# Scan and weighing: one operand moved into PSUM in both

## The chip, the cores and the metric

The kernel runs on one core of one Trainium2 chip. The metric is the device time of one execution in microseconds. Five engines work side by side, each through its own list of instructions in order: TensorE (PE, with its weight loads as PEld), VectorE (DVE), ScalarE (ACT), GpSimd (POOL) and SyncE (SP, which issues most transfers). They meet through semaphores. SBUF is the working memory, PSUM the eight banks that TensorE writes into.

## The reference

Eight images of 56x56 pixels with 128 channels pass through four layers. Layers 0, 2 and 3 are deformable convolutions: for each pixel, 9 points in 4 groups are sampled from a table of projected pixels, each with 4 bilinear corners, weighted by corner and softmax mask, summed, projected, normalized, and sent through an MLP:

```
offset = (h @ w_off + b_off); mask = softmax(h @ w_msk + b_msk)
samp = sum over 4 corners of img[idx] * weight
y = einsum('nghwpc,nhwgp->nhwgc', samp, mask) @ w_out + b_out
x = x + gamma1 * layer_norm(y); x = x + gamma2 * layer_norm(mlp(x))
```

Layer 1 is a selective scan in four directions over the 3,136 pixels, with 256 channels (two halves of 128) and 16 states:

```
h = h * exp(dt * A) + (dt * u) * B
y = sum over the 16 states of h * C
```

## The kernel before

**Two strands of work.** The 24 stages (three deformable layers for eight images) and the scans of the eight images run interleaved. A planner writes one list of items before anything runs (`Planner`, `schedule`); each engine goes through that list and emits its share of each item. The planner alternates one weighing with some scan ticks at a fixed pace and places everything else (projections, depthwise convolutions, the MLP chain of pixel pairs) by lags counted in ticks. There is no other scheduling: an engine that waits holds up all that stands behind it in its list.

**A stage.** Pixels come in 25 tiles of 128. For each tile 36 points are gathered from a table in DRAM by GpSimd's indirect transfers (L730), one for each point, 128 rows of 128 numbers each (4 corners of 32 channels). Twelve of them form a third of a tile and fill one of five slots `d_g`. VectorE weighs a third when it has landed (L1325), in three instructions of four points, each gather times its weight `d_wt`, broadcast over 32 channels. TensorE then sums the 12 points and corners of the third by 24 matmuls with the identity into `d_p` (L1014; item `sum`, placed behind the first scan tick after the weighing). That frees the slot for GpSimd. A 24-point pair of tiles goes on through the MLP chain (item `ch`: L1188 to L1218 on TensorE, L1563 to L1587 on VectorE).

**The scan.** An image has 448 steps: 28 pieces (direction, stretch of 448 pixels) times 16 states. Each step has a tick `s`. For step S the decay exp(dt*A) is made by ScalarE for the first half of the channels into a PSUM bank (`dA0` in `l_pm`, L781) and for the second half into SBUF (`dA1`, three buffers). TensorE spreads the step's row of B over the partitions into bank `l_pb` and the row of C into `l_pc` (L965, one matmul each). VectorE's tick for step S, in order:
- L1288: scan of the first half, 448 pixels, decay from PSUM.
- L1290: scan of the second half, first 224 pixels, all operands in SBUF.
- L1301: `dtu` times B's row for step S+1, both halves, 896 elements, into one of four buffers `hb`. It frees `l_pb`.
- L1305: scan of the second half, last 224 pixels.
- L1311: `hb` of step S-1 times C's row, 896 elements. It frees `l_pc`.

TensorE's tick S: row of B for S+1 (item `sB`), row of C for S-1, then the accumulation of `hb` of step S-2 by four matmuls into `l_acc` (L996). ScalarE's tick saves the last column of step S-1 (`carry`, L762), makes dA1 for S+2 and dA0 for S+1. After the ticks of an image come items of its output (`g`, `m`) and the projection of the next one (`p`).

Of the kernel before, what the change touches and what calls it, by code (L numbers as in the profile page):

```python
# [10 lines left out]
ALU = mybir.AluOpType  # L11
# [7 lines left out]
C = 128  # L19
# [53 lines left out]
def vss_ticks(n, order):  # L73

    out = [(0.0, [("need", order.index((0, 0)))])] + after_scan(-1, n)
    for i in range(n):
        for c in range(2):
            for h in range(2):
                out += [(0.5, [("c", i, c, h, part)]) for part in range(3)]
        out += [(0.3, [("h", i, 0, m)]) for m in range(9)]  # L80
        for sig in range(-1, NSTEP + 3):
            tick = [("sB", i, sig - 1)] * (0 <= sig < NSTEP) + [("s", i, sig)]
            j, q = divmod(sig, 16)
            if 0 <= sig < NSTEP:
# [260 lines left out]
def bank_uses(item):  # L345
# [21 lines left out]
    if kind == "s":  # L367
        _, i, sig = item
        s = NSTEP * i + sig
        if sig == -1:  # L370
            return [("pb", ("B", s + 1))]
        return [("pc", ("C", s - 1))] if 1 <= sig <= NSTEP else []
    if kind == "sB":
        _, i, sig = item
        return [("pb", ("B", NSTEP * i + sig + 2))] if sig + 2 < NSTEP else []
# [22 lines left out]
class Mem:  # L398


    def __init__(self, sb, ps, dram, n):
# [82 lines left out]

        self.dA0, self.dA1 = self.pm[:, 0:448], [wk[5][:, 0, :], wk[5][:, 1, :], wk[6][:, 0, :]]
# [26 lines left out]
class Job:  # L512


    def __init__(self, n, order, plan, mem, sems, a, out):
# [11 lines left out]
        self.total = total  # L527

# [217 lines left out]
def scalar_program(e, J):  # L746
# [211 lines left out]
def tensor_program(e, J):  # L958
# [17 lines left out]
    for item in J.plan:  # L976
        kind = item[0]
        if kind == "s":
            _, i, sig = item
            S = NSTEP * i + sig  # L980
            if sig == -1:
# [16 lines left out]
        elif kind == "sB":  # L998
            _, i, sig = item
            if sig + 2 < NSTEP:  # L1000
                row_of_B(NSTEP * i + sig + 2)
# [224 lines left out]
def vector_program(e, J):  # L1226
# [30 lines left out]
    for item in J.plan:  # L1257
        kind = item[0]
        if kind == "s":
# [17 lines left out]
            if 0 <= sig < NSTEP:  # L1277
# [5 lines left out]
                way, one, two, mid = slice(None), slice(0, 224), slice(224, 448), 223  # L1283
                if kd >= 2:
                    way, one, two, mid = slice(None, None, -1), slice(447, 223, -1), slice(223, None, -1), 224
                e.wait_ge(s["f_pb"], J.free("B", S))
# [20 lines left out]
            if 1 <= sig <= NSTEP:  # L1307
                x = S - 1
                e.wait_ge(s["p_pc"], J.full("C", x))
                e.wait_ge(s["ca"], x + 1)  # L1310
                e.tensor_tensor(m.hb[x % 4][:, :, :], m.hb[x % 4][:, :, :], bc(m.pc[:, 0:448], 1, 2),  # L1311
                                ALU.mult).then_inc(s["f_pc"], 1)
        elif kind == "weigh":
# [232 lines left out]
        elif kind == "ch":  # L1546
# [48 lines left out]
         "dA0 dA1 s1h sh ca accd d1 d2 hd0 md m2 lo ab ex uu qq s1 ln pag psq xir brd lag lsq xmr gsq gt gb tg").split()  # L1595
# [106 lines left out]
```

## Time and profile before

| | us |
|---|---|
| median of 3 runs | 31,024.93 |
| lowest, highest | 30,998.21, 31,036.17 |
| span of the profiled execution | 31,070.8 |
| VectorE busy | 23,050.6 (74%) |
| TensorE busy | 23,014.3 (74%) |
| GpSimd busy | 23,383.1 (75%) |
| ScalarE busy | 12,015.2 (39%) |

The profiled execution is the span and is 46 us over the median of the runs. Busy time counts instructions, not the issue time between two gathers, so GpSimd's share is to be read with its idle time beside it. The first scan tick starts at about 1,605 us and the last ends at about 28,258 us; before and after there are only stages.

### The profile page before, as it was taken

Reading aid. Unit: us, or ns where it says so; the run is one execution under the profiler, and the core shown is the slowest. Engines: PE = TensorE matmul, PEld = TensorE weight load, DVE = VectorE, ACT = ScalarE, POOL = GpSimd, SP = SyncE. Lnnn points to the kernel's source line nnn. Section 1 sums busy time; section 2 is a strip of 40 time slices with the busy share of each in tenths; the row PEclk is TensorE's granted clock in tenths of the full one; section 3 lists DMA queues with packets and bytes.
Section 4 is the critical chain, followed back from the end, with each engine's and each line's share of the span. In section 5 each row is a group of like instructions: output and inputs, shape, how many; then the busy total and the mean of one; then the engine's idle time right before and its main releaser. Section 6 shows DMA issues by size and latency. Waiting matters only on the chain.

```text
span 31070.8 us, 287429 instructions
## 1 busy us (share of the span) xinstructions
PE 23014.3 (74%) x94224; PEld 14570.5 (47%) x94224; DVE 23050.6 (74%) x38816; ACT 12015.2 (39%) x20358; POOL 23383.1 (75%) x21172
## 2 busy tenths in 40 slices
PE   5578778787787778777877787777877787777444
PEld 4444445444544454444544454444544454435433
DVE  1289887888588868888788859886788858885212
ACT  1144444444344434443444434443444444433000
POOL 6777777777677777777777767777677777656767
PEclk7788889888888888888988889888888888888666
DMA  3212122221221221212222121212222121112221
GB/s 75 75 50 64 54 66 65 57 64 51 71 61 51 64 73 51 64 50 57 70 58 63 49 72 53 59 51 64 58 58 61 50 72 52 51 42 67 64 57 53
DMA packets 2410662, 1854.55 MB, mean 60 GB/s; under 512 B 1686546, under 2 KB 2045508, under 8 KB 2409164
## 3 DMA queue, kind: packets, MB, share of 16 engines
q0 software_dynamic: 677376, 1388.62, 16.1%
q1 hardware_dynamic: 1731788, 447.55, 6.5%
q8 instruction: 745, 12.21, 0.2%
q14 instruction: 753, 6.17, 0.1%
HBM read 1569.35 MB, written 265.21 MB: 59 GB/s over the span
## 4 chain that ended last, share of the span: by engine, by line
POOL 61%; issue 18%; PE 12%; DVE 6%; ACT 2%; DMA 1%; SPq 1%; DVEq 0%; POOLq 0%; ACTq 0%
POOL d_g L730 61%; PE d_p L1014 2%; PE d_pr L1162 2%; DVE l_wk L1311 1%; PE l_acc L996 1%; DVE l_wk L1288 1%; DVE d_g L1325 1%; PE d_pr L1049 1%; PE l_pc L1127 1%; DVE l_wk L1305 1%; PE d_pr L1216 1%; DMA d_xin<-mid 0%; SPq L629 0%; DVE l_wk L1290 0%; PE d_pr L1209 0%
## 5 line engine op out<-in xcount | busy, mean ns | idle before, releaser
L730 POOL DMA_INDIRECT d_g<-table,d_idx x21168 | 23382.9, 1105 | 7645.0 <-issue 6426.9
L1014 PE MATMUL d_p<-d_g,c_ident 128*128 128x128 f32 x43200 | 6292.8, 312 | 2702.1 <-DVE d_g L1325 2697.1
L1014 PEld LDWEIGHTS d_p<-d_g,c_ident 128*128 128x128 f32 x43200 | 6108.4, 226 | 3849.1 <-DVE d_g L1325 2820.6
L996 PE MATMUL l_acc<-l_wk,c_ident 128*128 128x448 f32 x14336 | 7295.8, 639 | 436.7 <-DVE l_yx L1276 348.4
L1325 DVE TENSOR_TENSOR d_g<-d_g,d_wt 128x512 f32<-128x512 f32 x5304 | 3361.9, 689 | 3335.2 <-DMA d_g<-table,d_idx 3333.1
L781 ACT ACTIVATE l_pm<-l_wk,l_a 128x448 f32<-128x448 f32 x3584 | 2272.9, 634 | 7292.9 <-DVE l_wk L1288 7287.8
L1301 DVE TENSOR_TENSOR l_wk<-l_wk,l_pb 128x896 f32<-128x896 f32 x3584 | 3824.5, 1067 | 1501.6 <-PE l_pb L965 1499.4
L996 PEld LDWEIGHTS l_acc<-l_wk,c_ident 128*128 128x128 f32 x14336 | 3176.0, 223 | 2507.2 <-issue 2334.0
L1311 DVE TENSOR_TENSOR l_wk<-l_wk,l_pc 128x896 f32<-128x896 f32 x3584 | 3808.2, 1063 | 25.3 <-ACT l_carry L762 21.1
L1288 DVE TENSOR_TENSOR_SCAN l_wk<-l_pm,l_carry,l_wk 128x448 f32<-128x448 f32 x3072 | 3505.4, 1141 | 4.2 <-ACT l_pm L781 1.6
L1305 DVE TENSOR_TENSOR_SCAN l_wk<-l_wk 128x224 f32<-128x224 f32 x3584 | 2432.1, 679 | 0.3
L781 ACT ACTIVATE l_wk<-l_wk,l_a 128x448 f32<-128x448 f32 x3584 | 2362.2, 659 | 17.1 <-DVE l_wk L1357 3.0
L965 PE MATMUL l_pc<-l_spl,c_sel 96*128 96x448 bf16 x3584 | 1424.5, 397 | 1190.4 <-DVE l_wk L1311 1184.1
L1290 DVE TENSOR_TENSOR_SCAN l_wk<-l_wk,l_carry 128x224 f32<-128x224 f32 x3072 | 2026.0, 659 | 0.0
L965 PE MATMUL l_pb<-l_spl,c_sel 96*128 96x448 bf16 x3584 | 1400.9, 391 | 670.5 <-DVE l_wk L1301 668.7
L762 ACT ACTIVATE l_carry<-l_wk 128x2 f32<-128x2 f32 x3584 | 725.9, 203 | 2695.8 <-DVE l_wk L1305 2689.5
L781 ACT ACT_TABLE_LOAD x1181 | 1515.2, 1283 | 21.2
L1162 PE MATMUL d_pr<-d_xt,d_diag 128*128 128x448 f32 x3024 | 1358.5, 593 | 33.9 <-ACT d_xt L889 27.0
L1216 PE MATMUL d_pr<-d_fc,d_ht 128*128 128x128 f32 (+1 forms) x4800 | 903.8, 347 | 546.3 <-ACT d_ht L950 546.2
L965 PEld LDWEIGHTS l_pc<-l_spl,c_sel 96*128 96x128 bf16 x3584 | 369.2, 103 | 1902.7 <-DVE l_wk L1311 1754.3
L1216 PEld LDWEIGHTS d_pr<-d_fc,d_ht 128*128 128x128 f32 (+1 forms) x4800 | 771.6, 242 | 768.5 <-ACT d_ht L950 712.8
L965 PEld LDWEIGHTS l_pb<-l_spl,c_sel 96*128 96x128 bf16 x3584 | 370.2, 103 | 1597.6 <-DVE l_wk L1301 1104.1
(178 smaller groups left out, 22691.0 us busy)
## 6 DMA issues: line engine op xcount, KB each, us to landing
d_g<-table,d_idx POOLq DMA_INDIRECT x21168
table<-d_pst SPq DMA_DIRECT2D x2376, 64.0 KB
hd<-d_hst SPq DMA_DIRECT2D x168, 224.0 KB
d_htc<-hd SPq DMA_DIRECT2D x144, 256.0 KB
d_xin<-mid SPq DMA_DIRECT2D x112, 224.0 KB
mid<-d_xo SPq DMA_DIRECT2D x192, 128.0 KB
d_xres<-mid SPq DMA_DIRECT2D x192, 128.0 KB, 2.2
d_xin<-in_x SPq DMA_DIRECT2D x56, 224.0 KB
```

The costliest lines, as they stand in the source:

```text
L730: e.indirect_dma_start(out=m.g[Q % SLOTS][:, j, :], out_offset=None, in_=m.table[k % 2], in_offset=bass.IndirectOffsetOnAxis(ap=m.idx[G % ...
L781: e.activation(m.dA0 if h == 0 else m.dA1[x % 3], m.dt[P % 2][:, h, :], ACT.Exp, scale=m.aa[:, kd, h, n:n + 1]).then_inc(s[f"dA{h}"], 1)
L965: return e.matmul(bank[:, 0:448], m.sel[:, row + n:row + n + 1].to_broadcast([96, 128]), m.spl[P % 2][:, :], start=True, stop=True)
L996: ins = e.matmul(m.acc[:, h, 0:448], m.ident[:, :], m.hb[x % 4][:, h, :], start=(n == 0), stop=(n == 15))
L1014: ins = e.matmul(m.p0[:, t % 2 * 128:t % 2 * 128 + 32 * w], m.ident[:, :], m.g[Q % SLOTS][:, w * p:w * p + w, 32 * r:32 * r + 32], start=( ...
L1216: e.matmul(bank[0:n, i * 128:i * 128 + 128], m.ht[:, f, i * n:i * n + n], m.fc2[:, f, :], start=(f == 0), stop=False)
L1288: e.tensor_tensor_scan(hb[:, 0, way], m.dA0[:, way], hb[:, 0, way], ini[0], ALU.mult, ALU.add).then_inc(s["sh"], 1)
L1290: e.tensor_tensor_scan(hb[:, 1, one], dA1[:, one], hb[:, 1, one], ini[1], ALU.mult, ALU.add).then_inc(s["s1h"], 1)
L1301: e.tensor_tensor(m.hb[x % 4][:, :, :], m.dtu[P % 2][:, :, :], bc(m.pb[:, 0:448], 1, 2), ALU.mult).then_inc(s["f_pb"], 1)
L1305: e.tensor_tensor_scan(hb[:, 1, two], dA1[:, two], hb[:, 1, two], hb[:, 1, mid:mid + 1], ALU.mult, ALU.add).then_inc(s["sh"], 1)
L1311: e.tensor_tensor(m.hb[x % 4][:, :, :], m.hb[x % 4][:, :, :], bc(m.pc[:, 0:448], 1, 2), ALU.mult).then_inc(s["f_pc"], 1)
L1325: ins = e.tensor_tensor(g, g, wt, ALU.mult)
```

## The change

The second half's scan becomes one instruction of 448 that reads its input from B's bank `l_pb` in PSUM. For that the product of step S+1 is made in two instructions: the first half goes into `hb` as before, the second half is written over B's row in `l_pb`. The bank is free again only when that scan has read it. VectorE's order in a tick is now: scan of the first half, scan of the second half, product by C (S-1), two products by B (S+1). TensorE's item `sB` is gone: the tick spreads C's row for S-1 first, then B's row for S+1, then accumulates.

For a weighing that is the first after a scan tick (and whose weights were ready when that tick was written), ScalarE copies the weights of the third, 128x48, into the unused columns 448 to 496 of the bank `l_pm` at the end of its tick. VectorE weighs the third in one instruction of 1,536 elements with the weights read from there. Other weighings stay as they are.

```diff
-            tick = [("sB", i, sig - 1)] * (0 <= sig < NSTEP) + [("s", i, sig)]
+            tick = [("s", i, sig)]
...
+        self.wps = self.pm[:, 448:496]
...
+    def find_weights_in_psum(self):
+
+        self.copied, self.from_psum = {}, {}
+        step, ready = None, set()
+        for item in self.plan:
+            if item[0] == "s":
+                step, ready_then = item[1:], set(ready)
+            elif item[0] == "pr" and item[3] == 11:
+                ready.add(item[1:3])
+            elif item[0] == "weigh" and step and 0 <= step[1] < NSTEP - 1 and step not in self.copied:
+                if (item[1], item[2] // 4) in ready_then:
+                    self.copied[step] = item[1:]
+                    self.from_psum[item[1:]] = len(self.copied)
...
ScalarE, tick:
-                e.wait_ge(s["sh"], 2 * S)
+                e.wait_ge(s["sh"], S)
+                e.wait_ge(s["f_pb"], J.free("B", S - 1))
...
+            if (i, sig) in J.copied:
+                k, t, u = J.copied[i, sig]
+                G = 7 * k + t // 4
+                w = 4 * THIRDS[t][u]
+                e.wait_ge(s["wtr"], G + 1)
+                e.activation(m.wps[:, 0:w], m.wt[G % 2][:, t % 4, 12 * u:12 * u + THIRDS[t][u]].rearrange("p j r -> p (j r)"),
+                             ACT.Copy).then_inc(s["wps"], 1)
...
TensorE, tick:
-            if sig == -1:
-                row_of_B(S + 1)
             if 1 <= sig <= NSTEP:
                 if J.use["C", S - 1]:
                     e.wait_ge(s["f_pc"], J.use["C", S - 1])
                 spread(S - 1, m.pc, 16).then_inc(s["p_pc"], 1)
+            if sig + 1 < NSTEP:
+                row_of_B(S + 1)
...
VectorE, tick:
+                row = m.pb[:, 0:448]
+                e.wait_ge(s["bm"], 2 * S + 1)
                 e.wait_ge(s["dA0"], S + 1)
                 e.tensor_tensor_scan(hb[:, 0, way], m.dA0[:, way], hb[:, 0, way], ini[0], ALU.mult, ALU.add).then_inc(s["sh"], 1)
+                e.wait_ge(s["bm"], 2 * S + 2)
                 e.wait_ge(s["dA1"], S + 1)
-                e.tensor_tensor_scan(hb[:, 1, one], dA1[:, one], hb[:, 1, one], ini[1], ALU.mult, ALU.add).then_inc(s["s1h"], 1)
+                e.tensor_tensor_scan(hb[:, 1, way], dA1[:, way], row[:, way], ini[1], ALU.mult, ALU.add).then_inc(s["f_pb"], 1)
...
                 e.wait_ge(s["p_pb"], J.full("B", x))
-                e.tensor_tensor(m.hb[x % 4][:, :, :], m.dtu[P % 2][:, :, :], bc(m.pb[:, 0:448], 1, 2),
-                                ALU.mult).then_inc(s["f_pb"], 1)
-            if 0 <= sig < NSTEP:
-                e.wait_ge(s["s1h"], S + 1)
-                e.tensor_tensor_scan(hb[:, 1, two], dA1[:, two], hb[:, 1, two], hb[:, 1, mid:mid + 1],
-                                     ALU.mult, ALU.add).then_inc(s["sh"], 1)
+                e.tensor_tensor(m.hb[x % 4][:, 0, :], m.dtu[P % 2][:, 0, :], m.pb[:, 0:448], ALU.mult).then_inc(s["bm"], 1)
+                e.tensor_tensor(m.pb[:, 0:448], m.dtu[P % 2][:, 1, :], m.pb[:, 0:448], ALU.mult).then_inc(s["bm"], 1)
...
VectorE, weighing:
+            if (k, t, u) in J.from_psum:
+                e.wait_ge(s["wps"], J.from_psum[k, t, u])
+            step = parts if (k, t, u) in J.from_psum else 4
+            for j in range(0, parts, step):
+                if (k, t, u) in J.from_psum:
+                    wt = bc(m.wps[:, 0:4 * parts], 2, 32)
...
                 ins = e.tensor_tensor(g, g, wt, ALU.mult)
```

## Rows read from the trace of the kernel before

**Rows 1.** The page, part 4: the chain that ended last, by engine.
```profile
POOL 61%; issue 18%; PE 12%; DVE 6%; ACT 2%; DMA 1%; SPq 1%; DVEq 0%; POOLq 0%; ACTq 0%
```

**Rows 2.** Busy time (count) of PE, PEld, DVE, ACT, POOL in the scan stretch, granted clock, DMA share, GB/s.
```profile
1605.00:28258.00 26653.00, 20676.05 (x83559) 12671.17 (x83559) 22063.76 (x35990) 11464.66 (x19471) 20323.44 (x17985) 0.86 0.22 59
```

**Rows 3.** Grouped instructions of GpSimd, scan stretch and tail: busy, mean ns | idle, releasers.
```profile
L730 POOL DMA_INDIRECT d_g<-table,d_idx x17985 | 20323.7, 1130 | 6329.8 <-issue 5459.4 <-DVE d_idx L1520 494.8 <-PE d_p L1014 375.6
L730 POOL DMA_INDIRECT d_g<-table,d_idx x2039 | 1957.4, 960 | 814.0 <-issue 619.0 <-DVE d_idx L1520 154.6 <-PE d_p L1014 40.4
```

**Rows 4.** Grouped instructions of VectorE in the scan stretch.
```profile
L1301 DVE TENSOR_TENSOR l_wk<-l_wk,l_pb 128x896 f32<-128x896 f32 x3583 | 3823.4, 1067 | 1497.6 <-PE l_pb L965 1495.4
L1311 DVE TENSOR_TENSOR l_wk<-l_wk,l_pc 128x896 f32<-128x896 f32 x3582 | 3806.0, 1063 | 23.0 <-ACT l_carry L762 21.1 <-PE l_pc L965 1.6
L1288 DVE TENSOR_TENSOR_SCAN l_wk<-l_pm,l_carry,l_wk 128x448 f32<-128x448 f32 x3072 | 3505.4, 1141 | 4.2 <-ACT l_pm L781 1.6
L1325 DVE TENSOR_TENSOR d_g<-d_g,d_wt 128x512 f32<-128x512 f32 x4513 | 2854.1, 687 | 1063.2 <-DMA d_g<-table,d_idx 1061.2
L1305 DVE TENSOR_TENSOR_SCAN l_wk<-l_wk 128x224 f32<-128x224 f32 x3584 | 2432.1, 679 | 0.3
L1290 DVE TENSOR_TENSOR_SCAN l_wk<-l_wk,l_carry 128x224 f32<-128x224 f32 x3072 | 2026.0, 659 | 0.0
```

**Rows 5.** Grouped matmuls of TensorE in the scan stretch.
```profile
L996 PE MATMUL l_acc<-l_wk,c_ident 128*128 128x448 f32 x14324 | 7291.0, 639 | 436.7 <-DVE l_yx L1276 348.4 <-DVE l_yx L1271 88.3
L1014 PE MATMUL d_p<-d_g,c_ident 128*128 128x128 f32 x35304 | 4805.5, 299 | 949.7 <-DVE d_g L1325 944.9
L965 PE MATMUL l_pc<-l_spl,c_sel 96*128 96x448 bf16 x3582 | 1423.8, 397 | 1190.4 <-DVE l_wk L1311 1184.1
L965 PE MATMUL l_pb<-l_spl,c_sel 96*128 96x448 bf16 x3582 | 1400.2, 391 | 670.1 <-DVE l_wk L1301 668.3
```

**Rows 6.** Timeline, 16,510 to 16,525 us: start, us, engine, instruction, idle before.
```profile
16510.46 0.68 DVE L1305 TENSOR_TENSOR_SCAN l_wk<-l_wk 128x224 f32<-128x224 f32 x1
...
16510.62 1.27 POOL L730 DMA_INDIRECT d_g<-table,d_idx  x1 [0.30 <-issue]
...
16515.36 1.14 DVE L1288 TENSOR_TENSOR_SCAN l_wk<-l_pm,l_carry,l_wk 128x448 f32<-128x448 f32 x1
...
16515.49 5.03 PE L1014 MATMUL d_p<-d_g,c_ident 128*128 128x128 f32 x24 [0.61 <-DVE d_g L1325]
...
16517.21 0.95 POOL L730 DMA_INDIRECT d_g<-table,d_idx  x1 [0.31 <-issue]
...
16520.71 1.14 DVE L1288 TENSOR_TENSOR_SCAN l_wk<-l_pm,l_carry,l_wk 128x448 f32<-128x448 f32 x1
...
16521.60 1.67 PE L996 MATMUL l_acc<-l_wk,c_ident 128*128 128x448 f32 x4
...
16524.90 1.14 DVE L1288 TENSOR_TENSOR_SCAN l_wk<-l_pm,l_carry,l_wk 128x448 f32<-128x448 f32 x1
```

**Rows 7.** Timeline, 10,004 to 10,017 us.
```profile
10004.28 2.84 PE L1014 MATMUL d_p<-d_g,c_ident 128*128 128x128 f32 x24
...
10015.60 1.08 DVE L1349 SCALAR_TENSOR_TENSOR l_wk<-l_wk 128x896 f32<-128x896 f32 x1
...
10015.77 3.55 POOL L730 DMA_INDIRECT d_g<-table,d_idx  x1 [0.30 <-issue]
...
10016.60 1.89 DVE L1325 TENSOR_TENSOR d_g<-d_g,d_wt 128x512 f32<-128x512 f32 x3
```

**Rows 8.** Other forms, grouped over the whole span: VectorE, then ScalarE.
```profile
L1353 DVE TENSOR_TENSOR l_wk<-l_wk 128x896 f32<-128x896 f32 x224 | 243.0, 1085 | 0.1
L1271 DVE SCALAR_TENSOR_TENSOR l_yx<-l_xb,l_ds,l_acc 128x448 f32<-128x448 f32 x112 | 70.7, 673 | 0.0
...
L762 ACT ACTIVATE l_carry<-l_wk 128x2 f32<-128x2 f32 x3584 | 725.9, 203 | 2695.8 <-DVE l_wk L1305 2689.5
L781 ACT ACTIVATE l_pm<-l_wk,l_a 128x448 f32<-128x448 f32 x3584 | 2272.9, 634 | 7292.9 <-DVE l_wk L1288 7287.8
```

More of the change, by code:

```diff
@@ L369, in bank_uses @@
         s = NSTEP * i + sig
-        if sig == -1:
[L371 to L375, printed above, removed]
+        uses = [("pc", ("C", s - 1))] if 1 <= sig <= NSTEP else []
+        return uses + [("pb", ("B", s + 1))] if sig + 1 < NSTEP else uses
     if kind == "g":
@@ L527, in __init__ @@
         self.total = total
+        self.find_weights_in_psum()
+    def find_weights_in_psum(self):
[10 more added lines that the diff above has]
+                    self.from_psum[item[1:]] = len(self.copied)
     def tables(self, T):
@@ L777, in scalar_program @@
                 if h == 0 and x:
-                    e.wait_ge(s["sh"], 2 * x - 1)
+                    e.wait_ge(s["sh"], x)
                 if h == 1 and x >= 3:
-                    e.wait_ge(s["sh"], 2 * x - 4)
+                    e.wait_ge(s["f_pb"], J.free("B", x - 3))
                 e.activation(m.dA0 if h == 0 else m.dA1[x % 3], m.dt[P % 2][:, h, :], ACT.Exp,
                              scale=m.aa[:, kd, h, n:n + 1]).then_inc(s[f"dA{h}"], 1)
+            if (i, sig) in J.copied:
[5 more added lines that the diff above has]
+                             ACT.Copy).then_inc(s["wps"], 1)
         elif kind == "h":
@@ L980, in tensor_program @@
             S = NSTEP * i + sig
-            if sig == -1:
-                row_of_B(S + 1)
             if 1 <= sig <= NSTEP:
@@ L997, in tensor_program @@
                 ins.then_inc(s["accd"], 1)
[L998 to L1001, printed above, removed]
         elif kind == "sum":
@@ L1281, in vector_program @@
                 ini = [0.0 if c == (6 if kd >= 2 else 0) else m.carry[:, h, n:n + 1] for h in range(2)]
[L1283 to L1286, printed above, removed]
+                way = slice(None, None, -1) if kd >= 2 else slice(None)
+                row = m.pb[:, 0:448]
+                e.wait_ge(s["bm"], 2 * S + 1)
                 e.wait_ge(s["dA0"], S + 1)
                 e.tensor_tensor_scan(hb[:, 0, way], m.dA0[:, way], hb[:, 0, way], ini[0], ALU.mult, ALU.add).then_inc(s["sh"], 1)
+                e.wait_ge(s["bm"], 2 * S + 2)
                 e.wait_ge(s["dA1"], S + 1)
-                e.tensor_tensor_scan(hb[:, 1, one], dA1[:, one], hb[:, 1, one], ini[1], ALU.mult, ALU.add).then_inc(s["s1h"], 1)
+                e.tensor_tensor_scan(hb[:, 1, way], dA1[:, way], row[:, way], ini[1], ALU.mult, ALU.add).then_inc(s["f_pb"], 1)
+            if 1 <= sig <= NSTEP:
+                x = S - 1
+                e.wait_ge(s["p_pc"], J.full("C", x))
+                e.wait_ge(s["ca"], x + 1)
+                e.tensor_tensor(m.hb[x % 4][:, :, :], m.hb[x % 4][:, :, :], bc(m.pc[:, 0:448], 1, 2),
+                                ALU.mult).then_inc(s["f_pc"], 1)
             if sig + 1 < NSTEP:
@@ L1300, in vector_program @@
                 e.wait_ge(s["p_pb"], J.full("B", x))
-                e.tensor_tensor(m.hb[x % 4][:, :, :], m.dtu[P % 2][:, :, :], bc(m.pb[:, 0:448], 1, 2),
-                                ALU.mult).then_inc(s["f_pb"], 1)
-            if 0 <= sig < NSTEP:
-                e.wait_ge(s["s1h"], S + 1)
-                e.tensor_tensor_scan(hb[:, 1, two], dA1[:, two], hb[:, 1, two], hb[:, 1, mid:mid + 1],
-                                     ALU.mult, ALU.add).then_inc(s["sh"], 1)
[L1307 to L1312, printed above, removed]
+                e.tensor_tensor(m.hb[x % 4][:, 0, :], m.dtu[P % 2][:, 0, :], m.pb[:, 0:448], ALU.mult).then_inc(s["bm"], 1)
+                e.tensor_tensor(m.pb[:, 0:448], m.dtu[P % 2][:, 1, :], m.pb[:, 0:448], ALU.mult).then_inc(s["bm"], 1)
         elif kind == "weigh":
@@ L1321, in vector_program @@
             e.wait_ge(s[name], count)
-            for j in range(0, parts, 4):
-                g = m.g[Q % SLOTS][:, j:min(j + 4, parts)].rearrange("p j (r c) -> p (j r) c", c=32)
-                wt = bc(m.wt[G % 2][:, t % 4, 12 * u + j:12 * u + min(j + 4, parts)].rearrange("p j r -> p (j r)"), 2, 32)
+            if (k, t, u) in J.from_psum:
+                e.wait_ge(s["wps"], J.from_psum[k, t, u])
+            step = parts if (k, t, u) in J.from_psum else 4
+            for j in range(0, parts, step):
+                g = m.g[Q % SLOTS][:, j:min(j + step, parts)].rearrange("p j (r c) -> p (j r) c", c=32)
+                if (k, t, u) in J.from_psum:
+                    wt = bc(m.wps[:, 0:4 * parts], 2, 32)
+                else:
+                    wt = bc(m.wt[G % 2][:, t % 4, 12 * u + j:12 * u + min(j + 4, parts)].rearrange("p j r -> p (j r)"), 2, 32)
                 ins = e.tensor_tensor(g, g, wt, ALU.mult)
@@ L1594 @@
          "weighed accq ysa ytp yta idx wtr w0 pv py exd bst agg sqd x1r xor gbr dgr bsq bnr "
-         "dA0 dA1 s1h sh ca accd d1 d2 hd0 md m2 lo ab ex uu qq s1 ln pag psq xir brd lag lsq xmr gsq gt gb tg").split()
+         "wps dA0 dA1 bm sh ca accd d1 d2 hd0 md m2 lo ab ex uu qq s1 ln pag psq xir brd lag lsq xmr gsq gt gb tg").split()
 def program(nc, a, out, n_img=8, layers=(0, 1, 2, 3)):
```

## The prediction

> **What bounds the kernel now.** I read the chain of waits first: 61% of it is GpSimd's gathers and 18% the issue time between them [rows 1], so the reader should suspect GpSimd, not VectorE. Then three stretches: 0 to 1,605 us (no scans yet), 1,605 to 28,258 us (the 3,584 ticks of the scan beside the gathers), and the rest. In the middle one, the scan stretch, VectorE is busy 22,064 of 26,653 us, TensorE 20,676, GpSimd 20,323 [rows 2]. GpSimd looks freer than it is: its 17,985 gathers have 5,459 us of issue time between them (0.30 each) and only 870 us of real waits [rows 3]. It is 97% taken. A gather takes 1,130 ns there, but 960 ns in the tail, where VectorE does little [rows 3]. So something on VectorE lengthens it.
>
> The grouped instructions of VectorE say how little slack it has against GpSimd: it waits 1,061 us for gathers (1,063 idle in all) (before weighings) and 1,498 us for B's row from TensorE (before L1301) in this stretch [rows 4]. All three engines are within a few per cent of each other; that is the difficulty of this case.
>
> The timeline shows what lengthens gathers. One that starts 1.85 us into a tick, where the product L1301 with its row in PSUM runs, takes 0.95 us; one that meets L1305 takes 1.27 [rows 6], and one that meets L1349 and the three weighings takes 3.55 and ends within about 1 us of them [rows 7]. L1305, L1290, L1325 and L1349 have two SBUF inputs. Gathers wait for such instructions and not for those with an operand in PSUM.
>
> **Part 1, the weighings.** A weighing of 12 points is three instructions of 512 elements: 1.89 us [rows 7]. It becomes one of 1,536 with the weights in PSUM. Counted in the written order, 1,347 of 1,776 weighings qualify (one after each scan tick that has one); the rest lie at the stage ends, the head and the tail. Price: 896 elements take 1.067 us at L1301, 512 take 0.687 at L1325 and 896 all in SBUF 1.085 at L1353 [rows 4, 8], 1.03 ns an element, so 1.067 + 640 x 1.03 ns = 1.73 us. That saves 0.16 us, and with the seams between three instructions I take 0.2 x 1,347 = 270 us of VectorE (bounds: -100, if the repeated read from PSUM is slower than L1301's, to 300).
>
> ScalarE gets 1,347 copies of 128x48: between 0.20 us (128x2) and 0.63 (128x448) [rows 8], taken as 0.25, 340 us in all. They are queued behind dA0 of the next step, which starts when the first scan ends; VectorE has 3 us of its tick left then, and ScalarE is busy 11,465 of 26,653 us [rows 2]. I cost them at nothing; without that cover they would cost up to 340 us.
>
> **Part 2, the scan's second half.** Per tick L1290 and L1305 (0.659 + 0.679) become one scan of 448, which at L1288 takes 1.141 [rows 4]: -0.20. The product of 896 (1.067) becomes two of 448: 2 x (1.067 - 0.461) = 1.21 by the same slope, and at most 2 x 0.673 by L1271 [rows 8], +0.14 to +0.28, the second writing into PSUM, which no row shows. Instructions overlap by some 0.08 us, which takes a little off both. Sum -0.06 x 3,584 = -200 us (bounds -250 to +300; I take the near row's).
>
> A page would put these otherwise. The Trainium skill ("VectorE: DVE Perf Modes", the TRN2 errata section) gives instructions from PSUM a fixed cost 62 cycles above those from SBUF, 65 ns at 0.96 GHz. Here the opposite stands: L1311 with a PSUM operand takes 1.063, L1353 all in SBUF 1.085 [rows 4, 8], so the measurement decides; by the page the two parts would give back 0.065 x (3,584 + 1,347) = 320 us of the 470.
>
> **What GpSimd gets.** L1290, L1305 and nine tenths of L1325 no longer have two SBUF inputs; L1349, L1353 and their like stay. In the tail, where only weighings are of that kind, gathers take 0.96 us [rows 3]; beside a single L1305 they lose 0.32 [rows 6]. I bound the new mean of the stretch by 0.96 and 1.05, which frees 1,400 to 3,000 us of GpSimd over 17,985 gathers, and take the middle, 2,200. It then needs some 2,200 us less than the stretch is long, and is off the path. So VectorE loses its waits for gathers, 1,063 us. This is the purpose, and by itself it makes 1,063 + 270 + 200 = 1,530 us.
>
> **What it costs: B's row.** Before, the bank of B's row comes free at the end of the product L1301, and the next row is read a tick later after the first scans: TensorE may be a whole tick early. After, the bank carries the product and comes free only when the scan of the second half ends. Then TensorE (in order: C's row, B's row, the two accumulations, the sum of a weighing, pieces of convolutions and of the MLP) must write B's row while VectorE does one product by C (1.06 us). The row itself is hidden, 0.39 us [rows 5]. But everything queued behind it waits for that scan's end too, every tick, and TensorE can bank no lead. Behind it stand the accumulations, the sums (which free gather slots; five slots, so GpSimd bears that), and the chain of the MLP. And C's row, now ahead of B's, must be there before the product.
>
> So each tick costs the longer of TensorE's work between two B rows and VectorE's work; light ticks no longer pay for heavy ones. In the written order a weighing is always followed by a scan tick, and its sum of 24 matmuls comes in that next tick; 1,349 ticks have a sum and none of these has a weighing. TensorE's heavy ticks are VectorE's light ones.
> - TensorE in a tick with a sum, mean rows [rows 5]: B 0.39, accumulation 7,291/3,582 = 2.04, sum 4,806/1,471 = 3.27, C 0.40, the rest (20,676 less these four groups, over 3,584) 1.6: 7.7 us. At full clock: accumulation 1.67, sum 2.84 [rows 6, 7], the two rows 0.6 together and the rest 1.35 (estimates: the means of above at that clock, overlapping): 6.45.
> - VectorE in such a tick: 4.19 for the scan tick (16,520.71 to 16,524.90, a tick with nothing else in it) [rows 6], and 0.75 for the rest (22,064 less the groups of rows 4, over 3,584): 4.95.
> - The excess is 1.5 to 2.75 us. The example of rows 6 by hand: second scan ends at 17.5 instead of TensorE running free, B's row to 17.9, accumulation to about 20, sum to 23 to 25, L1209 and C's row to 24.1 to 26.2, where VectorE wants it at 22.8: 1.4 to 3.4 us late. Today that tick has no stall.
>
> I take the middle, 2.1 us x 1,349 = 2,830 us. Of today's 1,498 us of stalls I count half as lying on such ticks already and keep the other half, 750. Stalls after: 3,580, which is 2,080 more than today. The granted clock decides within this: 0.86 in the stretch [rows 2], and sums that follow a wait run at the lower of the two levels, 1.2 GHz (5.03 us, after a wait for the weighing [rows 6]), those behind other work at 2.4 (2.84 [rows 7]).
>
> **Sum.** +2,080 - 1,063 - 470 = +550 us on the profiled execution, whose span is 31,071 us; the median shown is 31,025, 46 lower, and I take the difference as it is: 31,570 less something for TensorE being found closer to its upper clock level once sums no longer wait for their weighing: **31,500 us**, about 1.5% slower. Head and tail (4,418 us) keep their SBUF weighings and do not change.
>
> **Rivals.**
> - Faster: the lead TensorE loses was not used. For it: GpSimd's relief is certain, and TensorE waits 1,184 us for L1311 before C's row [rows 5], so it has idle time somewhere. Against: that idle time lies in ticks without a sum and cannot be moved. If stalls stay at 1,498 us: 31,025 - 1,530 = 29,500; if they grow half as much, 30,500. The Trainium skill ("SBUF — State Buffer", on the port pair that VectorE and GpSimd share) has the rule by which only this gain would show: an instruction with two SBUF inputs locks GpSimd out for its whole length. The rows above agree on the lock; it says nothing of TensorE. Chance 0.33.
> - Near nothing: gain and stalls cancel at an excess of 1.7 us a tick: 31,000. Chance 0.13.
> - Much slower: the excess is 2.75 us and all of today's stalls remain: the stalls grow by 1,349 x 2.75 = 3,710 us, less 1,530: +2,180, 33,200. TensorE's waits in the MLP chain would have to be just as long as now although it comes later. Chance 0.10 for over 32,500.
> - The change frees nothing: gathers stay at 1.13 us because it is another thing that delays them. Then GpSimd keeps its 97%, and TensorE's stalls partly coincide with waits for gathers: -470 - 1,063 is not to be had in full, about 32,000. Chance 0.04, on the slower side.
> - Likeliest, 31,100 to 32,500: chance 0.40.
>
> The sign turns at one point: whether TensorE's tick with a sum exceeds VectorE's by more or less than 1.7 us. A measurement of this kernel can tell 0.2% (60 us) from no change. Faster 0.33, same 0.13, slower 0.54. The range for 8 in 10 is 29,900 to 32,500; the likeliest case alone has 31,100 to 32,300.
>
> **What would show it.** Gathers in the scan stretch at 1.00 us instead of 1.13; GpSimd with real waits of 2 ms or more, now for TensorE's sums (slots). Waits for gathers before weighings below 200 us. VectorE waiting 3 ms or more for B's and C's rows, mostly in the tick after a weighing. The one-instruction weighing at 1.73, the second scan at 1.14, the products at 0.60 each. Wrong if: waits for rows stay under 2,500 us (then it is faster), the product into PSUM takes over 0.8 us, or weighings wait for ScalarE's copy.

## The result, and where the time went

The changed kernel takes 32,746 us (median of 4 runs, 32,739 to 32,763) against 31,024 for the kernel before: a ratio of 1.0556 (95% interval 1.0541 to 1.0571). It is slower, as forecast, but by 1,720 us where I had 475, and outside the range.

The profiled execution has a span of 32,737.3 us. First the chain that ended last, by engine, from the page of the changed kernel; it answers to [rows 1].

```profile
PE 44%; DVE 30%; issue 13%; POOL 8%; ACT 4%; DMA 1%; SPq 1%; DVEq 0%; ACTq 0%; POOLq 0%
```

GpSimd's share went from 61% to 8%, and TensorE's from 12% to 44%. The scan stretch, now from 1,604 to 29,941 us, with the columns of [rows 2], and GpSimd's gathers in it, answering to [rows 3]:

```profile
1604.00:29941.00 28337.00, 21371.52 (x83525) 13092.33 (x83526) 21753.38 (x33316) 11575.74 (x20819) 17609.65 (x18022) 0.82 0.22 55
...
L742 POOL DMA_INDIRECT d_g<-table,d_idx x18022 | 17610.3, 977 | 10727.6 <-issue 5211.0 <-PE d_p L1030 4281.9 <-DVE d_idx L1538 1234.7
```

The gather fell from 1,130 to 977 ns, GpSimd's work in the stretch from 20,323 to 17,610 us, and its real waits rose from 870 to 5,517 us, most of them for slots that TensorE's sums free. All that the change did for GpSimd became idle time. Now VectorE's groups in the same stretch, answering to [rows 4]:

```profile
L1311 DVE TENSOR_TENSOR l_wk<-l_wk,l_pc 128x896 f32<-128x896 f32 x3582 | 3839.2, 1072 | 4465.3 <-PE l_pc L985 3644.1 <-ACT l_carry L775 817.9
L1303 DVE TENSOR_TENSOR_SCAN l_wk<-l_pm,l_carry,l_wk 128x448 f32<-128x448 f32 x3072 | 3498.2, 1139 | 4.5 <-ACT l_pm L794 1.7
L1306 DVE TENSOR_TENSOR_SCAN l_wk<-l_wk,l_carry,l_pb 128x448 f32<-128x448 f32 x3072 | 3437.1, 1119 | 0.0
L1343 DVE TENSOR_TENSOR d_g<-d_g,l_pm 128x1536 f32<-128x1536 f32 x1329 | 2314.0, 1741 | 8.8 <-ACT l_pm L801 6.5
L1324 DVE TENSOR_TENSOR l_pb<-l_wk,l_pb 128x448 f32<-128x448 f32 x3584 | 2224.3, 621 | 0.0
L1323 DVE TENSOR_TENSOR l_wk<-l_wk,l_pb 128x448 f32<-128x448 f32 x3583 | 2191.9, 612 | 17.0 <-PE l_pb L985 16.8 <-issue 0.2
```

The new instructions cost what the rows of before said: second scan 1.12 us, products 0.61 and 0.62, weighing 1.74. The product into PSUM is 9 ns dearer than the one into SBUF. What is new is 4,465 us of idle time before the product by C (L1311), where there were 23; the 1,498 us before the product by B (L1301) have become 17 (L1323). Who waits for whom, over the whole span of the changed kernel (engine, line, waited for: us, times, longest):

```profile
PE l_pb L985 <- DVE l_wk L1306: 5570.0, 2046, 10.6
...
POOL d_g L742 <- PE d_p L1030: 4355.2, 922, 43.6
DVE l_wk L1311 <- PE l_pc L985: 3651.0, 1249, 12.9
...
ACT l_wk L824 <- PE d_pr L1052: 1585.2, 424, 12.5
ACT l_bcd L812 <- PE d_pr L1044: 1290.7, 224, 12.7
```

TensorE waits 5,570 us for the second scan before it may write B's row, in 2,046 of 3,584 ticks; VectorE waits 3,651 us for C's row, in 1,249. Neither engine is full. Counted tick by tick in the trace, 1,356 of the 3,584 ticks have the sum of a weighing in TensorE's list between two C rows, and these carry 3,035 us of the waits for C's row; the other 2,228 ticks carry 616. Before the change the waits for B's row split into 868 and 627. So the new stalls lie where TensorE's tick is heavy and VectorE's light. The timeline shows one round of it (start, us, engine, instruction, idle before):

```profile
16515.43 1.11 DVE L1306 TENSOR_TENSOR_SCAN l_wk<-l_wk,l_carry,l_pb 128x448 f32<-128x448 f32 x1
...
16516.60 0.56 PE L985 MATMUL l_pb<-l_spl,c_sel 96*128 96x448 bf16 x1 [5.63 <-DVE l_wk L1306]
...
16516.95 3.19 PE L1016 MATMUL l_acc<-l_wk,c_ident 128*128 128x448 f32 x4
...
16519.79 1.12 DVE L1306 TENSOR_TENSOR_SCAN l_wk<-l_wk,l_carry,l_pb 128x448 f32<-128x448 f32 x1
...
16520.08 2.13 PE L1044 MATMUL d_pr<-l_xb,l_xp 128*40 128x448 f32 x4
...
16522.14 2.94 PE L1030 MATMUL d_p<-d_g,c_ident 128*128 128x128 f32 x24
16522.24 0.54 ACT L812 ACTIVATE l_bcd<-d_pr 40x448 f32<-40x448 f32 x1 [6.06 <-PE d_pr L1044]
...
16523.32 0.19 ACT L775 ACTIVATE l_carry<-l_wk 128x2 f32<-128x2 f32 x1
...
16524.92 0.35 PE L985 MATMUL l_pc<-l_spl,c_sel 96*128 96x448 bf16 x1
...
16525.31 1.09 DVE L1311 TENSOR_TENSOR l_wk<-l_wk,l_pc 128x896 f32<-128x896 f32 x1 [4.40 <-PE l_pc L985]
```

TensorE idles 5.63 us until the scan L1306 ends at 16,516.54. Only then come B's row, the accumulation at the lower clock level (granted clock 0.50 from 16,516.6 to 16,520; 3.19 us for what takes 1.67 at 1.00 [rows 6]), an item of the next piece's prelude (L1044, the projection from which the piece's rows of B and C come) and the sum. C's row is there at 16,525.27; VectorE had wanted it at 16,520.9. The same lines show a wait that I had not priced: ScalarE's list stands at L812 for TensorE's L1044 until 16,522.24, and `carry` (L775) stands behind it. The product by C needs `carry` too: it overwrites the `hb` of step S-1, whose last column `carry` saves.

The stretch closes by these terms: VectorE's time at work, overlaps counted once, -310 us (22,064 to 21,753); waits for gathers -1,057 (1,061 to 4); waits for rows +2,164 (1,497 to 3,661); waits for `carry` +797 (21 to 818); all other waits of VectorE, together, +90. Sum +1,684; head and tail -17; span +1,667.

One of these terms misleads. The profile puts a wait down to whatever ended it last. In 218 of the 302 ticks in which `carry` came last C's row was late too, and only some 255 of the 818 us lie after its arrival. Had `carry` always been in time, VectorE would have waited for C's row through the other 560 or so (worked out from the end times in the trace, not from a run).

### The profile page after: what moved, and what is told of

It reads as the page before. It is cut to its first block, busy times and chain, and to the rows that moved or that the text cites. A ratio compares the mean times of both kernels' runs of the same rounds, so it can differ in the third digit from the quotient of the medians.

```text
span 32737.3 us, 294488 instructions
## 1 busy us (share of the span) xinstructions
PE 23709.4 (72%) x94224; PEld 14986.9 (46%) x94224; DVE 22735.6 (69%) x36140; ACT 12125.6 (37%) x21705; POOL 20626.5 (63%) x21172
## 4 chain that ended last, share of the span: by engine, by line
PE 44%; DVE 30%; issue 13%; POOL 8%; ACT 4%; DMA 1%; SPq 1%; DVEq 0%; ACTq 0%; POOLq 0%
PE d_p L1030 13%; PE l_acc L1016 12%; POOL d_g L742 8%; DVE l_wk L1306 6%; DVE l_wk L1303 6%; DVE d_g L1343 4%; DVE l_wk L1323 3%; DVE l_wk L1311 3%; PE d_pr L1178 3%; PE l_pb L985 2%; PE d_pr L1065 2%; PE d_pr L1044 2%; PE d_pr L1232 1%; DVE l_pb L1324 1%; PE d_pr L1225 1%
## 5 line engine op out<-in xcount | busy, mean ns | idle before, releaser
L742 POOL DMA_INDIRECT d_g<-table,d_idx x21168 | 20626.3, 974 | 12068.1 <-issue 6166.5
L1016 PE MATMUL l_acc<-l_wk,c_ident 128*128 128x448 f32 x14336 | 8172.8, 705 | 0.0
L1030 PEld LDWEIGHTS d_p<-d_g,c_ident 128*128 128x128 f32 x43200 | 6327.5, 231 | 2924.3 <-DVE d_g L1343 1586.1
L1311 DVE TENSOR_TENSOR l_wk<-l_wk,l_pc 128x896 f32<-128x896 f32 x3584 | 3841.4, 1072 | 4472.3 <-PE l_pc L985 3651.0
L1016 PEld LDWEIGHTS l_acc<-l_wk,c_ident 128*128 128x128 f32 x14336 | 3477.3, 243 | 2164.0 <-issue 2005.4
L1306 DVE TENSOR_TENSOR_SCAN l_wk<-l_wk,l_carry,l_pb 128x448 f32<-128x448 f32 x3072 | 3437.1, 1119 | 0.0
L1343 DVE TENSOR_TENSOR d_g<-d_g,d_wt 128x512 f32<-128x512 f32 x1281 | 812.2, 688 | 2264.4 <-DMA d_g<-table,d_idx 2264.2
L1343 DVE TENSOR_TENSOR d_g<-d_g,l_pm 128x1536 f32<-128x1536 f32 x1347 | 2330.9, 1730 | 8.8 <-ACT l_pm L801 6.5
L1324 DVE TENSOR_TENSOR l_pb<-l_wk,l_pb 128x448 f32<-128x448 f32 x3584 | 2224.3, 621 | 0.0
L1323 DVE TENSOR_TENSOR l_wk<-l_wk,l_pb 128x448 f32<-128x448 f32 x3584 | 2192.5, 612 | 20.8 <-PE l_pb L985 20.7
L1232 PE MATMUL d_pr<-d_fc,d_ht 128*128 128x128 f32 (+1 forms) x4800 | 814.1, 322 | 238.2 <-ACT d_ht L970 236.1
L1584 DVE BATCH_NORM_STATS2 d_bs<-d_pr 128x6 f32<-128x128 f32 (+1 forms) x1200 | 294.4, 284 | 916.6 <-PE d_pr L1234 709.5
L1232 PEld LDWEIGHTS d_pr<-d_fc,d_ht 128*128 128x128 f32 (+1 forms) x4800 | 708.4, 223 | 445.0 <-ACT d_ht L970 365.7
```

Source lines behind the costliest of these rows:

```text
L742: e.indirect_dma_start(out=m.g[Q % SLOTS][:, j, :], out_offset=None, in_=m.table[k % 2], in_offset=bass.IndirectOffsetOnAxis(ap=m.idx[G % ...
L1016: ins = e.matmul(m.acc[:, h, 0:448], m.ident[:, :], m.hb[x % 4][:, h, :], start=(n == 0), stop=(n == 15))
L1030: ins = e.matmul(m.p0[:, t % 2 * 128:t % 2 * 128 + 32 * w], m.ident[:, :], m.g[Q % SLOTS][:, w * p:w * p + w, 32 * r:32 * r + 32], start=( ...
L1306: e.tensor_tensor_scan(hb[:, 1, way], dA1[:, way], row[:, way], ini[1], ALU.mult, ALU.add).then_inc(s["f_pb"], 1)
L1323: e.tensor_tensor(m.hb[x % 4][:, 0, :], m.dtu[P % 2][:, 0, :], m.pb[:, 0:448], ALU.mult).then_inc(s["bm"], 1)
L1324: e.tensor_tensor(m.pb[:, 0:448], m.dtu[P % 2][:, 1, :], m.pb[:, 0:448], ALU.mult).then_inc(s["bm"], 1)
```

## Experiments

The first four ran on one chip in one session, beside 31,029 us for the kernel before; the next four in another beside 31,014. "Row stalls" are VectorE's waits for B's or C's row over the span.

**The weighings alone** (e1_weights): the kernel before with this part of the change.

```diff
+        self.wps = self.pm[:, 448:496]
+            if (i, sig) in J.copied:   # ScalarE's copy, as in the change
-            for j in range(0, parts, 4):
+            step = parts if (k, t, u) in J.from_psum else 4
+            for j in range(0, parts, step):
```

> The kernel before with the weighings of the change alone (weights copied into PSUM, one instruction of 1,536); the scan and the order of TensorE are as before. My theory (the loss is the held bank of B's row and what TensorE loses by it): this part is a gain by itself. VectorE loses 0.16 us x 1,347 = 215 us of work, gathers fall from 1,130 to about 1,075 ns in the scan stretch, waits for rows stay near 1,500 us, VectorE's waits for gathers fall below 400 us: 29.9 to 30.6 ms. Rival (ScalarE's copies, or the read of the weights from PSUM, delay VectorE): 31.0 ms or more, with VectorE waiting for ScalarE before C's product by several hundred us.

Measured: 30,032 us, ratio 0.9684 (0.9667 to 0.9700). Gathers in its scan stretch and VectorE's weighings and products over the span:

```profile
L746 POOL DMA_INDIRECT d_g<-table,d_idx x17986 | 18859.8, 1049 | 6728.1 <-issue 5431.1 <-DVE d_idx L1549 719.2 <-PE d_p L1037 577.8
```

```profile
L1324 DVE TENSOR_TENSOR l_wk<-l_wk,l_pb 128x896 f32<-128x896 f32 x3584 | 3814.0, 1064 | 1593.2 <-PE l_pb L988 1590.4
L1334 DVE TENSOR_TENSOR l_wk<-l_wk,l_pc 128x896 f32<-128x896 f32 x3584 | 3794.2, 1059 | 36.4 <-ACT l_carry L778 23.6 <-PE l_pc L988 12.6
L1354 DVE TENSOR_TENSOR d_g<-d_g,l_pm 128x1536 f32<-128x1536 f32 x1329 | 2313.4, 1741 | 56.6 <-DMA d_g<-table,d_idx 43.0 <-ACT l_pm L804 7.6 <-issue 4.0
```

Half of the change is a gain of 3.2% by itself. Waits for gathers in the stretch fell to 90 us, row stalls stayed (1,603), ScalarE's copies cost 8 us of waits. The rival falls. The gathers' relief was larger than I expected (1,049, not 1,075 ns); why was not tested.

**The scan alone** (e2_scan): the changed kernel with the weighings of before.

```diff
         self.copied, self.from_psum = {}, {}
+        return
```

> The changed kernel with its weighings put back as they were before (three instructions from SBUF); only the scan's part of the change stays. My theory: the whole loss is here. Waits of VectorE before the product by C for C's row near 3,600 us and for ScalarE's carry near 800 us, as in the changed kernel; 32.8 to 33.3 ms, above the changed kernel, since the weighings cost 200 us more and lengthen gathers, though those are off the path. Rival (the weighings carry a good part of the loss): 31.5 to 32.3 ms.

Measured: 32,909 us, ratio 1.0608 (1.0591 to 1.0626). Row stalls 3,661, waits for `carry` 805, nearly as in the changed kernel (3,672 and 818). The whole loss is here, and with it in place the weighings are worth 160 us instead of 1,000: waits for gathers are down to 10 us in the stretch without them, so there is nothing left for them to save there.

**The hold alone** (e4_hold): the kernel before, VectorE untouched, TensorE made to write B's row after C's and not before the tick's first scan has ended.

```diff
-            if sig == -1:
-                row_of_B(S + 1)
...
                 spread(S - 1, m.pc, 16).then_inc(s["p_pc"], 1)
+            if sig + 1 < NSTEP:
+                if sig >= 0:
+                    e.wait_ge(s["sh"], 2 * S + 1)
+                row_of_B(S + 1)
```

> The kernel before with the hold alone: TensorE writes C's row first and then B's row, and B's row waits for the first scan (L1288) of the same tick. VectorE's instructions, their operands and the weighings are as before. My theory: VectorE's waits for rows rise from 1,500 to 3,500 us or more although no instruction of VectorE changed; its waits for gathers vanish (1,060 us); 31.8 to 32.8 ms. Rival (TensorE's lead was not used; the loss comes from the new instructions on VectorE): 31.0 to 31.2 ms.

Measured: 32,438 us, ratio 1.0453 (1.0435 to 1.0470). The same views, VectorE's group over the span and then the two waits:

```profile
L1295 DVE TENSOR_TENSOR l_wk<-l_wk,l_pb 128x896 f32<-128x896 f32 x3584 | 3873.6, 1081 | 3757.6 <-PE l_pb L961 3666.9
```

```profile
PE l_pb L961 <- DVE l_wk L1282: 4087.1, 1981, 9.6
DVE l_wk L1295 <- PE l_pb L961: 3666.9, 1405, 13.2
```

Not one instruction of VectorE is changed, and the stalls at B's row go from 1,499 to 3,667 us, 2,933 of them in ticks with a sum. Its waits for gathers in the stretch vanish as well (2 us), though nothing relieves GpSimd. The hold makes most of the loss: 1,409 us, where the whole scan part (e2_scan) loses 1,880. The edit also puts C's row ahead of B's, as the change does; the two were not tried apart. `carry` cost 19 us here. In this order VectorE waits for TensorE at the product by B and does one more scan before it wants `carry`; that this is what covers ScalarE's delay was only argued.

**The hold removed** (e3_two): e2_scan with two banks for B's row.

```diff
+def bank_of(x):
+    return ("pb", "pm")[x % 2]
-        self.dA0, self.dA1 = self.pm[:, 0:448], [...]
+        self.dA0, self.dA1 = wk[6][:, 1, :], [...]
-            e.wait_ge(s["f_pb"], J.use["B", x])
+            e.wait_ge(s["f_" + bank_of(x)], J.use["B", x])
-                row = m.pb[:, 0:448]
+                row = (m.pb, m.pm)[S % 2][:, 0:448]
```

> e2_scan with two banks for B's row, pb for even and pm for odd steps; dA0 moves from pm into SBUF to make room, so the first scan has two SBUF inputs and the second one operand in PSUM. VectorE's order and TensorE's order are those of e2_scan; only the wait of B's row for the scan of the same tick becomes one for the scan a tick earlier. My theory: VectorE's waits for rows fall from about 3,600 to under 1,500 us and the wait for the carry to under 200; gathers are longer again (about 1,110 ns) and GpSimd bounds: 30.5 to 31.2 ms. Rival (VectorE's new order, two long scans and then C's product, needs C's row too early whatever the banks do): waits before C's product stay over 3,000 us and the time over 32 ms.

Measured: 30,217 us, ratio 0.9741 (0.9725 to 0.9757), below the range that I gave. Gathers, and the product by C, over the span:

```profile
L747 POOL DMA_INDIRECT d_g<-table,d_idx x21168 | 22384.2, 1057 | 7778.7 <-issue 6410.8
...
L1316 DVE TENSOR_TENSOR l_wk<-l_wk,l_pc 128x896 f32<-128x896 f32 x3584 | 3811.6, 1064 | 1502.9 <-PE l_pc L990 1174.1
```

VectorE's list is the one of e2_scan; only where the first scan's decay lies and which scan B's row waits for differ. 2,690 us come back. Row stalls are 1,188, fewer than before the change (1,503); in ticks with a sum they are 659 us. The wait for `carry` fell to 324, not under 200, where e1_weights has 24; so a part of it does not come from the hold, and which piece of the edit makes it was not tested. I had the gathers too long: 1,075 ns in the stretch, not 1,110. That one block of some 1.1 us a tick delays them less than two of 0.66 does not explain it: e8_merge below has one block too, and its gathers are no shorter than those of e1_weights.

**When TensorE is let go, and what is queued behind it** (e5_swap, e6_acc, e7_swap_acc): the changed kernel with VectorE's two scans exchanged; with the accumulation ahead of B's row; with both.

```diff
 VectorE (e5, e7)
+                e.wait_ge(s["bm"], 2 * S + 2)
+                e.wait_ge(s["dA1"], S + 1)
+                e.tensor_tensor_scan(hb[:, 1, way], ...).then_inc(s["f_pb"], 1)
                 e.wait_ge(s["dA0"], S + 1)
                 e.tensor_tensor_scan(hb[:, 0, way], ...).then_inc(s["sh"], 1)
 TensorE (e6, e7)
-            if sig + 1 < NSTEP:
-                row_of_B(S + 1)
             if 2 <= sig <= NSTEP + 1:
...
                 ins.then_inc(s["accd"], 1)
+            if sig + 1 < NSTEP:
+                row_of_B(S + 1)
```

> The changed kernel with VectorE's two scans exchanged: the second half's scan, which frees the bank of B's row, comes first in the tick, so TensorE is let go 1.06 us earlier while VectorE needs C's row and B's row at the same places as before. My theory (the loss is how late TensorE is let go, set against its work in a tick): the waits before C's product fall from 3,650 + 820 us by up to 1.06 us for each of the 1,249 late ticks, to 2,900 to 3,500 us together; 31.3 to 32.0 ms. Rival (TensorE's lower clock level makes the loss, not the time of release): stalls and time as in the changed kernel within 1%.

> The changed kernel with TensorE's accumulation of step S-2 (L1016, four matmuls) put ahead of B's row instead of behind it. Its work in a tick is the same, but less of it is queued behind the hold, and only B's row, wanted 1.06 us after C's, comes last. My theory: each late tick gains 0.4 to 1.0 us, stalls fall by 500 to 1,200 us, now split between C's product and the product by B: 31.5 to 32.3 ms. Rival (the same work between two releases gives the same stalls): within 0.5% of the changed kernel.

> Both of the above together. If they act on the same lateness one after the other, the gains add up: 30.7 to 31.4 ms, about the time of the kernel before. If one takes what the other would have taken: as the better of the two, 31.3 ms or more.

| kernel | us | ratio (95%) | C's row | B's row | carry |
|---|---|---|---|---|---|
| changed | 32,746 | 1.0556 | 3,651 | 21 | 818 |
| e5_swap | 31,438 | 1.0132 (1.0115 to 1.0149) | 2,589 | 17 | 613 |
| e6_acc | 31,692 | 1.0218 (1.0201 to 1.0235) | 1,766 | 1,196 | 403 |
| e7_swap_acc | 31,171 | 1.0046 (1.0030 to 1.0063) | 1,337 | 1,171 | 349 |

The last three columns are VectorE's waits in us over the span. Exchanging two neighbouring instructions on VectorE gives 1,308 us, the earlier accumulation 1,054. Both rivals fall as stated, though the mean granted clock rose along with the gain (0.807 in the changed kernel, then 0.821, 0.827 and 0.831), so the clock may have a share. Together the two edits give 1,575 us rather than 2,362. The time lies in the range that I gave for gains that add up, but they do not: in part one takes what the other would.

**A version that beats both** (e8_merge): e1_weights, and the second scan as one instruction from SBUF; the bank of B's row comes free at the product, as before.

```diff
-                e.tensor_tensor_scan(hb[:, 1, one], dA1[:, one], hb[:, 1, one], ini[1], ...).then_inc(s["s1h"], 1)
+                e.tensor_tensor_scan(hb[:, 1, way], dA1[:, way], hb[:, 1, way], ini[1], ...).then_inc(s["sh"], 1)
...
-                e.tensor_tensor_scan(hb[:, 1, two], dA1[:, two], hb[:, 1, two], hb[:, 1, mid:mid + 1],
-                                     ALU.mult, ALU.add).then_inc(s["sh"], 1)
```

> A version meant to beat all: the kernel with the weighings alone (e1_weights), and the second half's scan in one instruction of 448 from SBUF instead of two of 224; the product by B stays one of 896 into SBUF, so the bank of B's row is freed as early as before. VectorE saves about 0.2 us a tick, 700 us; gathers meet one block of 1.1 us instead of two of 0.66, mean in the scan stretch 1,050 to 1,090 ns, which GpSimd now has room for. By my theory 29.3 to 29.7 ms. If GpSimd bounds again: about 30.0 ms with waits for gathers back at 500 us or more.

Measured: 29,842 us, ratio 0.9620 (0.9603 to 0.9636), the fastest of all, but above my range. VectorE's work in the stretch fell by 382 us against e1_weights, not 700 (I had added up durations that overlap), and waits for gathers rose from 90 to 392: GpSimd bounds again in part (40% of the chain that ended last, 18% in e1_weights). The gathers did not get shorter with the merged scan: 1,057 ns in the stretch, 1,049 in e1_weights.

**The merged scan alone** (e9_merge_alone, e10_merge_alone_again, e11_merge_again): whether merging pays without the weighings. The edit is the one above on the kernel before; e11 is e8_merge again.

> The kernel before with the second half's scan in one instruction of 448 from SBUF, weighings as before (three from SBUF). VectorE saves 0.11 us a tick, 390 us, as e8_merge did against e1_weights. My theory: without the weighings in PSUM GpSimd still bounds, so the saving turns into waits for gathers: 30.85 to 31.1 ms, waits for gathers in the scan stretch 1,200 us or more. Rival (VectorE's work is worth its full length anyway): 30.6 ms.

> The same kernel as e9_merge_alone, since that one ran on a chip where the kernel before itself took 35.7 ms instead of 31.0 and GpSimd was not the bound (134 us of waits for gathers in all), so it could not tell the two theories apart. My theory: with the kernel before at 31.0 ms GpSimd bounds and the saving of 390 us turns into waits for gathers: 30.85 to 31.1 ms. Rival (VectorE's work is worth its full length): 30.6 ms. If the kernel before is again at 35 ms: 0.985 to 0.99 of it, as last time.

> The same kernel as e8_merge, beside the one above on one chip. Where GpSimd bounds the kernel before (31.0 ms): 29.8 ms, ratio 0.962 as last time. Where the kernel before takes 35 ms, GpSimd is no bound and only VectorE's saved work counts, about 600 us: ratio 0.975 to 0.985.

Measured: 35,239 us beside 35,671 for the kernel before (0.9875, 0.9844 to 0.9905); 34,927 beside 35,346 (0.9891, 0.9874 to 0.9907); e11_merge_again 34,631 beside the same (0.9803, 0.9764 to 0.9842). The ratios are those that I had stated for a kernel before of 35 ms, but they are inconclusive for the question. The kernel before itself took 14 to 15% more in these two sessions, and VectorE's grouped instructions of e10 show idle time whose end the profile puts on nothing on this core ("remote"):

```profile
L1299 DVE TENSOR_TENSOR l_wk<-l_wk,l_pb 128x896 f32<-128x896 f32 x3584 | 3825.2, 1067 | 4917.2 <-remote 3339.6 <-PE l_pb L965 1093.6 <-issue 481.7
...
L1288 DVE TENSOR_TENSOR_SCAN l_wk<-l_wk,l_carry 128x448 f32<-128x448 f32 x3072 | 3450.8, 1123 | 0.0
...
L1319 DVE TENSOR_TENSOR d_g<-d_g,d_wt 128x512 f32<-128x512 f32 x5304 | 3327.1, 682 | 143.5 <-DMA d_g<-table,d_idx 140.5 <-issue 0.8
```

With 140 us of waits for gathers GpSimd was no bound there, so the case in which I wanted to test it did not arise. The longest of the "remote" waits in the timeline of e10:

```profile
24034.57 0.35 PE L965 MATMUL l_pb<-l_spl,c_sel 96*128 96x448 bf16 x1
...
24086.36 1.09 DVE L1299 TENSOR_TENSOR l_wk<-l_wk,l_pb 128x896 f32<-128x896 f32 x1 [50.83 <-remote]
```

B's row is recorded as written at 24,034.92, but the semaphore that VectorE waits for rises only at 24,086.33; from 24,037.2 until then only GpSimd's gathers run. In the traces of the kernel before and of e8_merge this signal follows the row by 0.014 us (median) and is more than 2 us behind only twice in 3,584 rows; in e10 it is so 783 times, by 6,043 us in all. So signals came late there, and what delays them stays open. e11's ratio of 0.980 beside the 0.962 of e8_merge fits a gain that is in good part GpSimd's relief; it does not show it.

## Why the prediction was right in kind and wrong in size

**What bounds the kernel now: right.** The weighings alone, which relieve GpSimd and save VectorE some work, brought 1,000 us, and 971 of them are waits for gathers (1,061 to 90).

**Part 1: right.** One instruction of 1.74 us for 1.73. VectorE's work in the stretch fell by 223 us in e1_weights for an expected 270. "I cost them at nothing", said of ScalarE's copies, holds: VectorE waited 8 us for them.

**Part 2, the work of VectorE: a term mis-sized.** I had -200 us. VectorE's work in the stretch, overlaps counted once, fell by 118 in e2_scan (22,064 to 21,946). Both parts together made 310, not 470. The single durations were right: added up, the changed scans and products give -190. The rest is overlap between neighbours, of which e2_scan has less than the kernel before. An instruction that starts after a wait overlaps nothing, and VectorE has 2,420 such starts in e2_scan against 1,820 before; whether that is all of it was not worked out. The higher fixed cost for operands in PSUM that the Trainium skill states ("VectorE: DVE Perf Modes", the TRN2 errata section) did not show here: the second scan, with its input in PSUM, took 1.119 us, and the merged one of e10, all in SBUF, 1.123.

**GpSimd's relief: right in size, but not what ended the waits.** 2,714 us less work in the stretch for an expected 1,400 to 3,000, waits for gathers 4 us for an expected "below 200". But e4_hold brings them to 2 us, and gathers from 1,130 to 1,058 ns, with every instruction of VectorE unchanged: a VectorE that is held up waits for no gathers anyway.

**B's row: the mechanism right.** e4_hold makes the stalls by the hold, e3_two removes them by a second bank. They lie where I had put them: 3,035 of 3,651 us in ticks with a sum. That I had 3,580 us and the profile says 3,661 is in part luck, since some 560 us more of waiting for C's row stand there as waits for `carry`. No run moved the sums by themselves.

**The step that failed: the size of the stalls, "I take the middle, 2.1 us x 1,349" with 750 kept, 3,580 in all.** Before its products VectorE waited 4,479 us in the stretch, for rows and for `carry`. By ticks, before the product by C: 3,497 us in the 1,356 ticks with a sum, 2.58 us each and not 2.1, and 972 us in the others, not 750. Two things are missing from that term.
- TensorE also feeds ScalarE (L1044, L1052 and the projections of the stages), and I did not ask who stands behind ScalarE when TensorE comes later. In the 302 ticks in which `carry` came last, ScalarE spent 1,865 of the 2,571 us between the end of the step's scans and `carry` waiting for TensorE's results. The sum has no term for this. By the profile's count it is 797 us, but only some 235 of them are `carry`'s own; through the rest C's row was late as well.
- The larger part, some 650 us, is thus TensorE's own lateness. I had even taken 70 us off because I expected TensorE nearer to its upper clock. It went the other way: 0.86 before, 0.82 after, and the accumulation, which now follows the pause of the hold, went from 639 ns a matmul [rows 5] to 706 in the stretch. Four of them are 0.27 us a tick, over 1,349 ticks some 360 us: an estimate of the clock's share, which no run separates.

The excess was also reckoned from a VectorE tick that rows 4 do not give as it is said: 22,064 less the six groups shown, over 3,584, is 1.01 us, not 0.75. Only with the two scans' other forms taken off as well (859 us, part of the 4.19 of a tick, but not shown) is it 0.77.

The 1,187 us by which the span missed are then 84 of waits put down to rows, 797 put down to `carry`, 160 of VectorE's work, 6 of waits for gathers, 90 for all other waits of VectorE (17 given back at head and tail), and the 70 taken off; the 3 left over are rounding.

**The rivals.** "Faster" had a third of the chance on the ground that TensorE's lead might be unused. It was used, as e4_hold shows: TensorE's waits of 668 us before B's row and 1,184 before C's [rows 5] were no proof of spare time. "Much slower" by its own terms (33,200) was nearer to the time than my forecast was, and so was its excess of 2.75 us to the 2.58 measured. But its condition, unchanged waits in the MLP chain, is not what happened: TensorE's wait for ScalarE's L950 before L1216 (L970 before L1232 after the change) fell from 535 to 224 us in the scan stretch.

## What to carry to other kernels

A bank is freed by its last reader: when a result is put over its own input in PSUM, ask how much earlier the bank was free before, and what stands in the writer's list behind the next write. Two engines that meet once a step cost the longer of their two times in every step, so where heavy steps of one are light steps of the other, a lead of one step, a second bank or an earlier release is worth more than the instructions themselves. When one engine is going to be late, go through every engine that it feeds, also those that are 40% busy. And when an instruction waits for two things, do not read the price of one off the profile's waits: ask when the other arrived.

## What the runs showed of the hardware

- Gathers by indirect DMA are held up by VectorE's instructions with two SBUF inputs and not by those with one operand in PSUM: in the scan stretch they took 1,130 ns before, 1,049 with most weights in PSUM (e1_weights), 1,011 with the second scan's input there (e2_scan), 977 with both. The summed length of such instructions is not all that counts: one scan of 1.12 us in e8_merge in place of two of together 1.34 left them at 1,057.
- A product written over its own PSUM operand took 0.62 us for 448 elements, 0.01 more than one written to SBUF.
- One kernel (e8_merge, e11_merge_again) took 29,842 us in one session and 34,631 in another on the same chip. VectorE was busy 22,444 and 22,493 us of it, with its product by B at 1,064 and 1,069 ns and gathers at 1,042 and 1,032. TensorE's accumulation went from 631 to 670 ns at a granted clock of 0.847 and 0.793. So nearly all of the difference is idle time of VectorE, and in e10, from the same session as the slower of the two, TensorE's signal to VectorE came late 783 times (above).
